# Score mask written into the PSUM bank by ScalarE instead of by a matmul with the identity

## What is computed

```
q = l2norm(q) * qs;  k = l2norm(k) * ksc          # then rotary
jt = concatenate([seq_p[:nw], seq_p[1:]], axis=1) # positions of the 64 keys, -1 before the first window
mask = (it < jb) | (it > jb + w) | (jb == -1)
sim = einsum('bhwie,bhwje->bhwij', bq, bk2) * QK_SCALE
sim = where(mask, -finfo.max, sim)
attn = softmax(sim, -1)
out = einsum('bhwij,bhwje->bhwie', attn, bv2)
```

## Time and profile before

| | |
|---|---|
| median of 3 executions | 3696.93 us (3695.18 to 3698.40) |
| profiled execution, its own time | 3698.82 us |
| its span, first to last instruction | 3697.0 us |
| mean granted TensorE clock | 0.975 of 2.4 GHz |
| before the six layers (modulation, full attention) | about 343 us of the span |
| mask matmuls (L755) | 384, 150.9 us busy |

### The profile page before, as it was taken

How to read it: one execution, slowest core, us unless ns; L and a number is a source line. 1 busy time by engine, 2 the same in 40 slices (tenths; PEclk the granted TensorE clock), 3 DMA queues, 4 the chain that set the end, 5 groups by cost and what they waited for, 6 DMA issues and landing times.

```text
span 3697.0 us, 132440 instructions
## 1 busy us (share of the span) xinstructions
PE 3426.7 (93%) x50548; PEld 2640.8 (71%) x50548; DVE 2640.4 (71%) x5823; ACT 2508.1 (68%) x5117; POOL 2356.0 (64%) x1568
## 2 busy tenths in 40 slices
PE   5666999999999999999999999999999999999997
PEld 4444877777777777777777777777777777777774
DVE  3445877777877777877777877777877777877773
ACT  2224766677777777777777776777776777777774
POOL 1004866667767667767667766667766667767662
PEclk9888999999999999999999999999999999999998
DMA  2000111121111121111121111121111121111111
GB/s 79 0 0 12 48 37 44 37 63 41 50 36 44 39 61 43 47 36 44 41 59 44 47 36 44 39 61 43 47 36 44 41 59 44 47 36 44 41 39 44
DMA packets 98169, 156.71 MB, mean 42 GB/s; under 512 B 18129, under 2 KB 39633, under 8 KB 96721
## 3 DMA queue, kind: packets, MB, share of 16 engines
q1 hardware_dynamic: 93440, 132.73, 13.3%
q10 hardware_dynamic: 4176, 15.74, 1.3%
HBM read 20.48 MB, written 2.10 MB: 6 GB/s over the span
## 4 chain that ended last, share of the span: by engine, by line
PE 77%; issue 6%; ACT 5%; POOL 1%; DVE 1%; ACTq 0%; DMA 0%; DVEq 0%; POOLq 0%; SPq 0%
PE psum L736 19%; PE psum L760 11%; PE psum L826 9%; PE psum L846 7%; PE psum L783 6%; PE psum L803 4%; PE psum L791 4%; PE psum L866 4%; PE psum L878 3%; PE psum L871 3%; PE psum L755 2%; PE psum L857 1%; PE psum L853 1%; ACT probT L553 1%; ACT aoT L510 1%
## 5 line engine op out<-in xcount | busy, mean ns | idle before, releaser
L377 POOL TENSOR_TENSOR qkr<-qks,rnorm 128x1024 f32<-128x1024 f32 x384 | 731.3, 1904 | 371.0 <-issue 291.1
L369 POOL TENSOR_TENSOR qks<-work 128x1024 f32<-128x1024 f32 x384 | 908.0, 2365 | 72.1 <-DVE work L1042 67.8
L385 POOL TENSOR_TENSOR probn<-prob,psumr 128x512 f32<-128x512 f32 x384 | 400.5, 1043 | 506.4 <-DVE psumr L1068 506.4
L536 ACT ACTIVATE sq<-psum 128x512 f32<-128x512 f32 x768 | 463.9, 604 | 346.9 <-PE psum L736 346.3
L736 PE MATMUL psum<-whi,xhi 128*128 128x512 f32 x1152 | 565.1, 491 | 107.0 <-issue 67.2
L1016 DVE TENSOR_REDUCE ssq<-sq 128x8 f32<-128x512 f32 x768 | 515.6, 679 | 48.6 <-ACT sq L536 12.2
L1040 DVE TENSOR_TENSOR work<-psum,rot 128x512 f32<-128x512 f32 x768 | 507.4, 661 | 58.6 <-POOL qks L369 43.3
L1074 DVE TENSOR_REDUCE nmax<-psum 128x8 f32<-128x512 f32 x384 | 264.9, 690 | 335.9 <-PE psum L760 334.6
L760 PEld LDWEIGHTS psum<-kT,qbd 128*64 128x64 f32 x12288 | 403.8, 142 | 109.9 <-issue 109.9
L760 PE MATMUL psum<-kT,qbd 128*64 128x64 f32 x12288 | 458.6, 230 | 0.9 <-issue 0.8
L736 PE MATMUL psum<-whi,xlo 128*128 128x512 f32 x1152 | 458.7, 398 | 0.0
(11 more groups left out here) (131 smaller groups left out, 6490.3 us busy)
## 6 DMA issues: line engine op xcount, KB each, us to landing
vsh<-vtok SPq DMA_DIRECT2D x384, 192.0 KB, 2.5
vsh<-vtok SPq DMA_DIRECT2D x384, 64.0 KB, 3.1
xsh<-xs_in SPq DMA_DIRECT2D x192, 64.0 KB, 2.0
ff_x<-x_mid SPq DMA_DIRECT2D x96, 128.0 KB
wqkv<-Wqkv_dram ACTq DMA_DIRECT2D x5, 1536.0 KB, 7.7
wo_next<-Wo_dram ACTq DMA_DIRECT2D x5, 512.0 KB, 8.3
xtok<-x_dram SPq DMA_DIRECT2D x4, 512.0 KB, 11.0
out_dram<-qkr SPq DMA_DIRECT2D x8, 256.0 KB, 2.5
```

The lines of the kernel that those rows point to most:

```text
L369: pool.tensor_tensor(qks[:, :, :], rcos, rsin, ALU.add).then_inc(s["add_ready"], 1)
L377: pool.tensor_tensor(qkr[:, j % 2, :, :], qks[:, :, :], rnorm[:, :].unsqueeze(2).to_broadcast([P, 2 * OCT, DH]), ALU.mult).then_inc(s["qkr ...
L385: pool.tensor_tensor(probn[:, :, :], prob[:, j % 2, :, :], psumr[:, j % 2, 1, :].unsqueeze(2).to_broadcast([P, OCT, KEYS]), ALU.mult).then ...
L536: act.activation(sq[:, w * OCT:(w + 1) * OCT, :], bank[w].rearrange("p (h n) -> p h n", n=DH), ACT.Square).then_inc(s[("sqq_ready", "sqk_r ...
```

## The change

ScalarE gets a new stage, `mask_seeded`, with lag 3, called in each pass right behind `ffn_square` and ahead of `x_high`. It waits for `sub_ready` of the unit before (for the very first unit, for `bits_set`), and copies the mask, broadcast over the four pairs, into bank 3. TensorE's `scores` loses the mask matmul and the wait for `sub_ready` and gets a wait for `seed_ready`; its first small matmul has `start=False`, as before. One matmul ahead of all turns writes the mask once with `start=True`, so that the bank's written flags are set.

```diff
+                    def mask_seeded(j):
+                        if j is None:
+                            return
+                        if first and j == 0:
+                            act.wait_ge(s["bits_set"], 1)
+                        else:
+                            wait_apart(act, ("sub_ready", units + j))
+                        entry = 1 if j // UPT % TPI or j < 0 else (it % 2 if isinstance(it, int) else act.snap(it % 2))
+                        act.activation(bank[3].rearrange("p (a k) -> p a k", a=PAIRS),
+                                       mask[:, bass.ds(entry, 1), :, :].rearrange("p a b k -> p a (b k)").to_broadcast([P, PAIRS, 2 * KEYS]),
+                                       ACT.Copy).then_inc(s["seed_ready"], 1)
...
                             ffn_square()
+                        mask_seeded(t.unit(u, 3))
                         x_high(t.unit(u, 0))
                         k_turned(t.unit(u, 3))
...
                     def scores(j):
                         if j is None:
                             return
-                        ti, tp, oc = j // UPT % TPI, j // UPT % 2, j % UPT
+                        tp, oc = j // UPT % 2, j % UPT
                         need(pe, "qk_ready", units, j + 1)
-                        need(pe, "sub_ready", units, j, first)
-                        entry = 1 if ti or j < 0 else (it % 2 if isinstance(it, int) else pe.snap(it % 2))
-                        m = mask[:, bass.ds(entry, 1), :, :].rearrange("p a b k -> p a (b k)").to_broadcast([P, PAIRS, 2 * KEYS])
-                        pe.matmul(bank[3].rearrange("p (a k) -> p a k", a=PAIRS), ident_bf[:, :], m,
-                                  start=True, stop=False, skip_group_check=True)
+                        need(pe, "seed_ready", units, j + 1)
...
             pe.wait_ge(s["pad_ready"], 1)
+            pe.matmul(bank[3].rearrange("p (a k) -> p a k", a=PAIRS), ident_bf[:, :],
+                      mask[:, 0:1, :, :].rearrange("p a b k -> p a (b k)").to_broadcast([P, PAIRS, 2 * KEYS]),
+                      start=True, stop=True, skip_group_check=True).then_inc(s["bits_set"], 1)
             attention()
```

More of the change, by code:

```diff
@@ L182, in build @@
             wqkv_in wo_in w1_in w2_in
-            sqq_ready sqk_ready ssq_ready ssk_ready sg_ready ln_ready rn_ready rotq_ready rotk_ready add_ready qkr_ready trq_ready trk_ready
+            sqq_ready sqk_ready ssq_ready ssk_ready sg_ready ln_ready rn_ready rotq_ready rotk_ready add_ready qkr_ready trq_ready trk_ready seed_ready bits_set
             q_ready qk_ready sim_ready max_ready sub_ready p_ready pt_ready pts_ready vp_ready vs_ready pv_ready
```

## The result

The changed kernel takes 3730.5 us (median of 4, 3726.4 to 3734.0) where the kernel before takes 3697.7 (median of 4): 1.0089 times as long, 95% interval 1.0071 to 1.0106. The forecast was 3636, faster by 61. It came out slower by 33.

A forecast was written before the change was run, and what follows sets the result against it. TensorE's matmul train, with one ScalarE stretch each turn, was taken as the bound. Masks saved 98.9 us, less 23.0 (pass 4), 7.7 (kT) and 7.2 (edges): 61.0, giving 3636 us; own range 3615 to 3655, 8 in 10 3594 to 3670.

The forecast's parts named there:

- 24 stalls "for no recorded reason": TensorE stands still 24 times without recorded reason, up to 3.8 us; listed, but given no term in the sum.
- Mask matmul, 0.32 us: Each mask matmul removed from TensorE's train saves 0.32 us, the distance between starts; ends 0.23 and 0.39.
- rival B: Mask cheaper than it looks: the first score matmul's weight load stands bare instead, 0.23 us per mask; 3664 us; chance 0.13.
- seven masks that the prediction held to be on the path: Pass 3's 48 masks gain nothing; after further exclusions 309 of 384 count on TensorE's path, 98.9 us.
- The seed, 0.48 us: Each ScalarE mask copy into PSUM puts what follows it back by 0.48 us; ends nothing and 1.11.
- pass 4 alone is uncovered: ScalarE is continuous from qbd to aoT and TensorE waits already, so the seed adds 48 x 0.48 = 23.0 us.
- the edges: Small slack limits, as in passes 5 and 7: 0.05 us on three passes a turn, 7.2 us lost.
- The 16 `kT` occasions: Where TensorE's weight load already waits for the kT copy, the seed adds 16 x 0.48 = 7.7 us.
- A straight turn was to fall by 1.3: Sign that the forecast is right: a full turn some 1.3 us shorter than 65.92.
- D: Slower, ScalarE becomes the bound: decides from a 0.97 us seed; at 1.11, 3719 us; chance 0.09, near side within 7 us 0.04.
- E: The change doesn't do what it says: non-zero seeds may not be added onto; no time and no chance of its own.
- "A granted clock that falls": Sign that the forecast is wrong: the granted clock falls in a full turn.

The follow-up runs named there:

- mask_out_only: The changed kernel without the ScalarE seeds, scores waiting for sub_ready again, so the mask is left out after the first unit: 3708.9 us, 1.0029 of the kernel before.
- after_pad64: The changed kernel with 64 small bf16 matmuls (128 instructions) ahead of all turns, which only move the code that follows: 3652.4 us, 0.9867 of the kernel before.
- seed_late_pad64: after_pad64 with the seed of pass 4 in feed-forward turns moved behind the copy into aoT: 3632.6 us, 0.9813 of the kernel before.
- seed_only: The kernel before plus the 384 ScalarE mask copies, written to a spare SBUF tile, mask matmul kept: 3745.3 us, 1.0122 of the kernel before.

## Why the prediction was wrong

**The step that failed** is not a term of the sum but one that it lacks. The prediction named the 24 stalls "for no recorded reason" among what stands still elsewhere, and gave them no term: it took them as unchanged. They are backward jumps, and they and what follows them hold the whole loss: 53 us over the 20 inner jumps, more than the net loss of 33, and 8.7 at the 4 jumps of the loop over layers. The changed kernel's inner target stands just ahead of a block's end, the earlier kernel's did not: 45 mask matmuls with their loads, some 90 instructions, were ahead of it. After 7 instructions TensorE waits for the next block, 28.3 us in 20 jumps, and the granted clock stands at 1.2 GHz for 140 us of these intervals in place of 37.5. The runs that show it leave the turns' instructions as they are: 3730.5, 3702.5, 3670.0, 3652.4, 3669.1, and 3730.6 again at a shift of 256.

**Mask matmul, 0.32 us.** Oversized: 0.23, which is the price of rival B and what the chain booked. The argument against B, that one bare load goes with the mask, was false in its result: one load stays bare either way, and it is the longer one (0.13 against 0.10). What the Trainium skill says in "TensorE: Matmul & The Clock Gate", section "Step-by-step: what each phase is for", that the queue pulls a weight load ahead of running matmuls, it says under a condition (other rows of the array, or a load into the background weights), which the prediction left out. For the mask's load before and the first score's load after, the trace shows no such lead: each starts with its matmul. `mask_out_only` against the kernel before gives 1.50 us a straight turn, 0.21 for each of the seven masks that the prediction held to be on the path.

**The seed, 0.48 us.** 0.52. That pass 4 alone is uncovered was right in the main: moving that one call saved 20 us by the medians, 25 by the wait. A straight turn pays 0.67 for all eight seeds (64.43 to 65.10), forecast 0.63 with the edges.

**The 16 `kT` occasions.** They became 58, but the matmul itself waited for `kT` 11 times as before, for 12.4 us in place of 7.0. The sum had 7.7 more, not far off.

**The sum.** A straight turn was to fall by 1.3. The turns 1 to 2 fell by 0.86, the turns 0 to 1 by 0.46. Over 48 turns that is an estimate of 22 to 41 us, in keeping with the 21 to 44 at equal positions; the forecast 61 was half as large again or more, even where jumps play no part.

**The rivals.** B had the right price for the mask and the wrong sign for the kernel. D had the right sign for the wrong reason: ScalarE is no bound, and `mask_out_only` is slower without it. The chance for slower, 0.09, stood for D alone; the 0.04 for its near side came on top, though the four chances were 1.00 already. E did not come about: the seeds, which are not 0, were added onto in all 384 units, and the changed kernel computes what the reference does. "A granted clock that falls" was listed as a sign, for a full turn; it fell, but behind the jumps.

**Left open.** Why the first hole has its minimum near 70 instructions and is longest near 46; the runs show that it goes by position and ends behind a packet, not why it takes 1.7 us or more from the landing. And the share of the clock: `after_pad64` and `seed_late_pad64` have the same TensorE code, and in the first layer's loop first holes of 3.3 and of 2.7 to 3.3 us, yet the former runs on at half clock for most of pass 0 (8.7 us to the pass's end, against 5.9). These four jumps alone are 12 us apart. No run separates fetch from clock there. Nor is it placed why `seed_only` pays 0.84 a straight turn, where the seed puts its follower back by 0.52.

## What to carry to other kernels

Where the trace shows a stall without releaser behind each backward jump of an engine, every edit of that engine's code is two edits: what it does, and where it puts the jump's target. Measure an edit in the straight parts of the trace, or at two or more positions of the code, before its time is believed; here position was worth 49 to 78 us, the edit 21 to 44. Count the packets of the instruction queue as well: one more block at each jump showed there at once. When a chain hands over to another engine for a stretch, put added work for that engine outside the stretch: here one moved call was worth 20 us, about half of the change.

## What the runs showed that was not expected

- The time is periodic in the position of the loops: 256 inserted instructions gave back the time (3730.5 and 3730.6, with single runs up to 11 us off) and the holes to the same place, within one instruction.
- The packets of the instruction queue are 16.4 KB. A block that ends some 7 instructions behind a jump's target costs a second hole of 0.5 to 2.2 us, one that ends 70 to 79 behind 0.3 to 1.3 where it shows, and one that ends 134 or more behind none.
- A restart of TensorE behind a jump came 1.65 to 2.70 us after an instruction packet had landed, in 336 of 336 cases.
- The first matmul behind the jump ran at half clock (0.79 us in place of 0.49) in 12 of 24 jumps of the changed kernel and in none before. The length of the hole does not decide it alone: of two holes of 3.77 us one was followed by 0.79 and one by 0.49.
- A ScalarE copy of 128 x 512 from bf16 in SBUF to PSUM takes 0.62 us, and its follower starts 0.52 later, against 0.48 behind copies out of PSUM. Into SBUF (`seed_only`) the same copy takes 0.64, and its follower starts 0.52 later too.
- Taking a bf16 matmul with 0.10 us of weight load out from ahead of an fp32 one gave 0.23 us, not its 0.32: the follower's load takes its place.
